# Second attention of a two-layer gated cross-attention kernel: q made transposed, its squares summed by one-column products, a new order in a unit, and the last stage merged into it

## The chip, the cores and the metric

The kernel runs on one core of one Trainium2 chip. The time is the device time of one execution in microseconds; smaller is better. The engines are PE (matrix products), DVE (vector), ACT (activations), POOL (GpSimd) and SP (which only issues transfers here). Each has its own queue of instructions and works it off in order; they wait for one another on semaphores.

## What is computed

Two layers, each a gated cross-attention and a gated feed-forward part, on x of 4 sequences x 256 tokens x 512 features:

```python
x = x + tanh(g_xattn[0]) * L0_xattn(layernorm(x), ctx)       # attn0
x = x + tanh(g_ffn[0])   * L0_ffn(layernorm(x))              # ffn0
x = x + tanh(g_xattn[1]) * L1_xattn(layernorm(x), ctx)       # attn1: changed
x = x + tanh(g_ffn[1])   * L1_ffn(layernorm(x))              # ffn1: moved

def L1_xattn(latents, ctx):                  # 32 heads, 8 key heads, head 128
    kv = concatenate([ctx, latents], 1)      # 64 + 256 keys
    q, k, v = latents @ Wq, kv @ Wk, kv @ Wv
    q, k = rms_norm(q, q_norm_w), rms_norm(k, k_norm_w)     # per head
    return softmax(q @ k.T / sqrt(128)) @ v @ Wo
def L1_ffn(x):                               # 28 experts of rank 8, top 2
    gate = softmax of the two largest of x @ gate_W.T
    return x @ base_W.T + ((x @ lora_A) * gate * 2) @ lora_B
```

All arithmetic is float32. Each operand of a large product is split into a part `hi` that the array's rounded format (fp32r) holds and a rest `lo`, and a product is the sum of three (`mm3`, lines 55 to 57: hi x lo, lo x hi, hi x hi).

## The kernel before

Four phases follow one another; each is a block in which every engine has its own program. The second attention (`attn1_phase`, line 861) has 8 key-head groups g (a loop on every engine, its first and last pass written out) and 4 sequences b, so 32 **units** n = 4g + b. A unit is one sequence with one key head and its four query heads. Units overlap: unit n does its own projections and scores, and in between the value and output products of unit n - 1.

The order of PE within a unit is written by hand (lines 1335 to 1409):

- k and v of 256 tokens, 24 products of 256 columns; for even b also k and v of the context of two sequences, 12 products (`cx`).
- `turn` 0 and 1: transpositions of the unnormalised probabilities p of unit n - 1; then q of the first 128 tokens, 12 products of 512 columns, with tokens as rows and the four heads as columns. `turn` 2 and 3, then q of the other 128 tokens. `turn` 4 and 5. A unit has 20 such 128x128 transpositions.
- `p_v(0)`: p times v for two heads, 8 products of 512 columns; the transpositions of k (2, in even units 3); four transpositions of q (line 1391); `p_v(1)`; the other four of q.
- scores 0 and 1 (12 products of 320 columns), output of the first 128 tokens (`out`, 12 of 512), scores 2, output of the other 128, scores 3.

A pair of scores j stands for 128 query tokens (`tile`) and two heads (`hp`); `PAIRS` gives the order, first both pairs of tile 0.

ACT copies each result out of PSUM as the `hi` part, and DVE subtracts to make the `lo` part, while the bank is held. q with tokens as rows is copied to `q_raw` by ACT (line 1215); DVE squares it and sums each head (`q_squares`, line 1023, eight instructions with a sum each), POOL takes the power -1/2 (lines 970 and 972), and PE transposes `q_raw`. The scale of q enters only in the exponential of ACT (line 1251) as the scale of each row, and in the negative row maximum `nb` (line 1034). k is squared and summed by DVE (line 1071), scaled after POOL's power (lines 964, 966, 1084), and transposed. The probabilities are divided by their sums in `scale_p` (line 1037), for the first pair by POOL (line 957).

The sequence of PSUM banks is fixed by `y_bank` and `x_bank`: two banks take turns for kv, cx, q, p times v and output, two for transposed things. A later product waits until the earlier content of its bank is split, or added into x (`x_add`, line 1013).

DVE and ACT also split the weights of the next group, in the last unit of a group (`w_kv`, `w_q`) and at the end of b = 0 and the start of b = 1 (`w_o`, `w_lo` and `w_hi`). The layer norm of tokens for the next phase is done in the last two units for tiles 0 to 3, and in `tail` for 4 and 5 (`ln_tiles`).

After the last unit, `tail` (line 1411) does the turns, p times v and output that are left. Then the block ends and `ffn1_phase` begins: splits of the base weights and of lora_B (lines 1508 to 1513, 1492), and for each of eight tiles the router and lora_A product (`ag`, 12 products of 256 columns), the base product (12 of 512), the routing on DVE (a chain of some twelve small instructions, lines 1527 to 1543), two transpositions of `hg` and six products of 512 columns with lora_B; DVE adds into x and SP stores.

Of the kernel before, what the change touches and what calls it, by code (L numbers as in the profile page):

```python
# [15 lines left out]


# [6 lines left out]
ALU = mybir.AluOpType  # L24
# [818 lines left out]
def attn1_buffers(k, scope, sb, pair):  # L843
    k.w_q, k.w_o = pair(scope, "w1q", [CH, GH * HD]), pair(scope, "w1o", [GH, HID])
    k.qT = pair(scope, "qT1", [2, GH, PART])
# [8 lines left out]
    k.q_raw, k.k_raw = sb(scope, "q_raw", [2, GH * HD]), sb(scope, "k_raw", [3, HD])  # L854
    k.p1 = sb(scope, "p1", [2, GH, SEQ + CTX])
    k.dump, k.rms_eps = sb(scope, "dump", [2 * GH + 3, HD]), sb(scope, "rms_eps", [2 * GH])
# [4 lines left out]
def attn1_phase(nc, k, sem, ln):  # L861


    def sems(*names):
# [5 lines left out]
    q_full, q_copied, pv_full, pv_hi, pv_split, d_full, x_added = sems(  # L870
        "q_full", "q_copied", "pv_full", "pv_hi", "pv_split", "d_full", "x_added")
    t_full, t_hi, t_split, kt_full, kt_hi, kt_split, qt_full, qt_hi, qt_split = sems(
        "t_full", "t_hi", "t_split", "kt_full", "kt_hi", "kt_split", "qt_full", "qt_hi", "qt_split")
    ssk_ready, rk_ms, rk_ready, k_scaled, ssq_ready, rq_ms, rq_ready = sems(
        "ssk", "rk_ms", "rk", "k_scaled", "ssq", "rq_ms", "rq")
# [7 lines left out]
    PAIRS = [(0, 0), (0, 1), (1, 0), (1, 1)]  # L883
# [18 lines left out]
    def x_bank(b, kind, j=0):  # L902
        at = {"t": j, "k": 6, "q": 7 + j}[kind]
        return bx[(9 * b + at) % 2]
# [7 lines left out]
    def ln_bank(b, i):  # L912
        return bx[(9 * b + 1 + i) % 2] if b < BATCH else bx[i]
# [10 lines left out]
    def stat(j):  # L924
        tile, hp = PAIRS[j]
        return slice(tile * GH + 2 * hp, tile * GH + 2 * hp + 2)

    def piece(kind, i):
        n = cols[kind] // CONV[kind]
        return slice(i * n, (i + 1) * n)  # L930

    def loop(eng, body, tail):

        body(0, True, True)
        with eng.Fori(1, NKV - 1) as g:
            body(g, False, True)
        body(NKV - 1, False, False)
        tail(NKV * BATCH)

    with nc.Block() as block:  # L940
        @block.sync
        def _(sp):
# [4 lines left out]
            for kind in ("kv", "q", "o"):  # L947
                sp.wait_ge(wlo[kind], NKV * CONV[kind])
                k.ffn1_load(sp, kind)

        @block.gpsimd
        def _(pool):
# [7 lines left out]
            def body(g, first, nxt):  # L960
                for b in range(BATCH):
# [8 lines left out]
                    pool.tensor_tensor(k.rq[:, :], k.ssq[:, :], k.rms_eps[:, :], ALU.add).then_inc(rq_ms, 1)  # L970
                    pool.wait_ge(rq_ms, n + 1)
                    pool.tensor_tensor(k.rq[:, :], k.rq[:, :], k.minus_half[:, 0:8], ALU.pow).then_inc(rq_ready, 1)
                    p_scale(n, 0)

            pool.memset(k.rms_eps[:, :], HD * RMS_EPS)
            pool.memset(k.ssk[:, :], 1.0).then_inc(stats_set, 1)
            def tail(n):
                for t in (4, 5):
                    ln.pool_rstd(pool, 3, t)
                for w in k.w_kv:  # L980
                    last = pool.memset(f(w[:, :].rearrange("p (c n) -> p c n", c=CH)[:, :, LR + NEXP:256]), 0.0)
                last.then_inc(k.ag_pad, 1)
# [4 lines left out]
        def _(dve):  # L987
            def w_lo(kind, g, i):
                s = piece(kind, i)
                dve.wait_ge(whi[kind], CONV[kind] * g + i + 1)  # L990
                dve.tensor_tensor(flat[kind][1][:, s], raw[kind][:, s], f(flat[kind][0][:, s]),
                                  ALU.subtract).then_inc(wlo[kind], 1)
# [20 lines left out]
            def x_add(n, b, j):  # L1013
                t = 2 * ((b - 1) % BATCH) + j
# [4 lines left out]
            def q_squares(n, b, tile):  # L1019
                dve.wait_ge(q_copied, 2 * n + tile + 1)  # L1020
                for h in range(GH):
                    q = k.q_raw[:, tile, h * HD:(h + 1) * HD]
                    last = dve.tensor_tensor_reduce(k.dump[:, tile * GH + h, :], q, q, 1.0, 0.0, ALU.mult, ALU.add,
                                                    k.ssq[:, tile * GH + h:tile * GH + h + 1])
                if tile == 1:
                    last.then_inc(ssq_ready, 1)
# [728 lines left out]
```

## Time and profile before

| | |
|---|---|
| median of 3 runs | 1496.01 us (1492.74 to 1496.33) |
| profiled execution, its own time | 1493.15 us |
| its span, first to last instruction | 1491.4 us |
| mean granted clock of PE | 0.992 |
| busy: PE, DVE, ACT, POOL | 1399.5, 1058.6, 798.0, 462.6 us |

The second attention takes from about 574 us to 1436 of the span, its 32 units up to 1410; the last stage the rest. A row of the timeline has the start and the duration in us, engine, line, operation, result and operands with their shape, and in brackets the idle time before it and what ended that. Durations of PE's products overlap. Where a helper issues an instruction, the row has the helper's line: all three-part products stand at lines 55 to 57 and are told apart by the names of their tiles.

### The profile page before, as it was taken

The page shows a single profiled execution, that of the slowest core. Times are in us where ns is not written, and L with a number is a line of the kernel's source. Part 1 is how long each engine was busy: PE and PEld are TensorE (multiplying, and loading weights), DVE is VectorE, ACT ScalarE, POOL GpSimd, SP SyncE. Part 2 cuts the span into 40 slices and gives each one's busy share as a digit, 9 for nine tenths or more (in the row PEclk, how much of TensorE's full clock was granted, in tenths as well). Part 3 has the DMA queues.
Part 4 walks back from the last instruction along what each step waited for, and adds up shares of the span by engine and source line. Part 5 has one row for each costly group of instructions (what it writes and reads, how often), then busy time and mean ns, then how long its engine had stood idle before and what let it go on. Part 6 is the DMA issues. An engine that isn't in the chain of part 4 may idle for free. (4 is left out here: it accounts for less than half of the span.)

```text
span 1491.4 us, 24301 instructions
## 1 busy us (share of the span) xinstructions
PE 1399.5 (94%) x7976; PEld 1199.3 (80%) x7976; DVE 1058.6 (71%) x2794; ACT 798.0 (54%) x2204; POOL 462.6 (31%) x588
## 2 busy tenths in 40 slices
PE   4999999998999998999999999999999999999889
PEld 4888888887778876888878888888888878887767
DVE  6777777778633337787787787787787777787765
ACT  4777777775211315565555555555555555555521
POOL 3855555554954612111111121111211111112120
PEclk8999999999999999999999999999999999999989
DMA  4111122111321301001001001001001000100001
GB/s 191 71 55 60 70 70 70 65 61 44 104 68 43 123 1 71 1 1 72 1 1 71 0 1 71 0 1 71 0 1 71 0 36 35 38 18 1 1 0 57
DMA packets 14958, 63.96 MB, mean 43 GB/s; under 512 B 1760, under 2 KB 1760, under 8 KB 10656
## 3 DMA queue, kind: packets, MB, share of 16 engines
q1 hardware_dynamic: 14880, 63.07, 11.8%
q8 instruction: 30, 0.49, 0.1%
q14 instruction: 48, 0.39, 0.1%
HBM read 60.97 MB, written 2.10 MB: 42 GB/s over the span
## 5 line engine op out<-in xcount | busy, mean ns | idle before, releaser
L1251 ACT ACTIVATE p<-psum,nb,rq 128x320 f32<-128x320 f32 x256 | 155.3, 614 | 161.8 <-DVE nb L1034 161.8
L55 PE MATMUL psum<-w1q_hi,xnT_lo 128*128 128x512 f32 x256 | 107.2, 419 | 12.8 <-DVE v_lo L1054 8.3
L964 POOL TENSOR_TENSOR rk<-ssk,rms_eps 128x3 f32<-128x3 f32 x32 | 6.3, 196 | 349.9 <-DVE ssk L1071 349.9
L999 DVE TENSOR_TENSOR pT_lo<-psum,pT_hi 128x512 fp32r<-128x512 f32 x128 | 88.1, 689 | 32.5 <-ACT pT_hi L1174 30.7
L1030 DVE TENSOR_REDUCE mx<-psum 128x2 f32<-128x640 f32 x128 | 105.0, 820 | 5.7
L1215 ACT ACTIVATE q_raw<-psum 128x512 f32<-128x512 f32 x64 | 38.3, 598 | 121.3 <-PE psum L57 121.3
L361 DVE TENSOR_TENSOR VW_lo<-psum,VW_hi 64x512 fp32r<-64x512 f32 x128 | 88.0, 688 | 19.1 <-ACT VW_hi L457 17.5
L57 PE MATMUL psum<-w1q_hi,xnT_hi 128*128 128x512 f32 x256 | 100.6, 393 | 0.0
L55 PE MATMUL psum<-w1o_hi,oT_lo 128*128 128x512 f32 x256 | 100.4, 392 | 0.0
L56 PE MATMUL psum<-w1o_lo,oT_hi 128*128 128x512 f32 x256 | 100.3, 392 | 0.0
L56 PE MATMUL psum<-w1q_lo,xnT_hi 128*128 128x512 f32 x256 | 99.8, 390 | 0.0
L57 PE MATMUL psum<-w1o_hi,oT_hi 128*128 128x512 f32 x256 | 99.7, 390 | 0.0
L957 POOL TENSOR_TENSOR p<-p,rinv 128x640 f32<-128x640 f32 x32 | 42.7, 1335 | 139.6 <-DVE rinv L1040 139.6
L481 ACT ACTIVATE p<-psum,nb 128x64 f32<-128x64 f32 x256 | 76.8, 318 | 16.7 <-DVE nb L393 16.4
L55 PE MATMUL psum<-w_kv_hi,xnT_lo 128*128 128x256 f32 x288 | 81.7, 284 | 3.1 <-PEq L687 1.8
L55 PE MATMUL psum<-kT_hi,qT_lo 128*128 128x320 f32 x256 | 81.9, 320 | 1.9 <-ACT p L1251 1.0
L1297 PE MATMUL psum<-ident,p 128*128 128x128 f32 x512 | 73.5, 277 | 10.0 <-DVE pT_lo L999 6.2
L457 ACT ACTIVATE VW_hi<-psum 64x512 fp32r<-64x512 f32 x128 | 75.9, 593 | 10.6 <-PE psum L57 8.6
L56 PE MATMUL psum<-w_kv_lo,xnT_hi 128*128 128x256 f32 x288 | 81.5, 283 | 0.0
L57 PE MATMUL psum<-w_kv_hi,xnT_hi 128*128 128x256 f32 x288 | 81.5, 283 | 0.0
L57 PE MATMUL psum<-kT_hi,qT_hi 128*128 128x320 f32 x256 | 79.1, 309 | 0.0
L56 PE MATMUL psum<-kT_lo,qT_hi 128*128 128x320 f32 x256 | 79.0, 309 | 0.0
(245 smaller groups left out, 4676.8 us busy)
## 6 DMA issues: line engine op xcount, KB each, us to landing
raw_q<-in_w0q SPq DMA_DIRECT2D x8, 1024.0 KB, 4.8
raw_o<-in_w0o SPq DMA_DIRECT2D x8, 1024.0 KB, 4.8
raw_q<-in_w1q SPq DMA_DIRECT2D x8, 1024.0 KB, 7.5
raw_o<-in_w1o SPq DMA_DIRECT2D x8, 1024.0 KB, 4.8
raw_kv<-in_w_gu SPq DMA_DIRECT2D x10, 512.0 KB, 3.6
raw_gu<-in_w_gu SPq DMA_DIRECT2D x10, 512.0 KB, 3.6
raw_kv<-in_w0kv SPq DMA_DIRECT2D x8, 515.0 KB, 3.3
raw_kv<-in_w1kv SPq DMA_DIRECT2D x8, 512.0 KB, 5.5
```

Source lines behind the costliest of these rows:

```text
L55: pe.matmul(out, w[1], m[0], start=start, stop=False)
L56: pe.matmul(out, w[0], m[1], start=False, stop=False)
L57: return pe.matmul(out, w[0], m[0], start=False, stop=stop)
L361: last = dve.tensor_tensor(k.VW[1][r, h // 2, 2 * pr + bp, :], bank[64 * bp:64 * bp + 64, :], f(k.VW[0][r, h // 2, 2 * pr + bp, :]), ALU.s ...
L457: last = act.activation(k.VW[0][r, h // 2, 2 * pr + bp, :], bank[64 * bp:64 * bp + 64, :], ACT.Copy)
L481: last = act.activation(k.p0[:, s % 4, h * CTX:(h + 1) * CTX], s_bank[s % 2][:, h * CTX:(h + 1) * CTX], ACT.Exp, bias=k.nb0[:, s % 2, h:h ...
L957: pool.tensor_tensor(p, p, k.rinv[:, stat(j)].unsqueeze(2).to_broadcast([PART, 2, KEYS]), ALU.mult).then_inc(p_scaled_pool, 1)
L999: last = dve.tensor_tensor(k.pT[1][:, kt, 2 * hp:2 * hp + 2, :], bank.rearrange("p (h q) -> p h q", h=2), f(k.pT[0][:, kt, 2 * hp:2 * hp + ...
L1030: dve.tensor_reduce(k.mx[:, stat(j)], s_pair(j), AX.X, ALU.max).then_inc(mx_ready, 1)
L1215: act.activation(k.q_raw[:, j // 2, :], y_bank(b, "q", j // 2)[:, :], ACT.Copy)\
L1251: last = act.activation(k.p1[:, tile, h, :], s_pair(j)[:, h % 2, :], ACT.Exp, bias=k.nb[:, i:i + 1], scale=k.rq[:, i:i + 1], accum_out=k.r ...
L1297: last = pe.transpose(bank[:, (2 * hh + tile) * PART:(2 * hh + tile + 1) * PART], k.p1[:, tile, 2 * hp + hh, CTX * hh + kt * PART:CTX * hh ...
```

## The change

In the second attention:

- **q is made transposed.** The weights of a head are now the stationary operand and the tokens move: 48 products of 256 columns for the 24 of 512 (`q_proj`), by pairs of heads. ACT copies the result straight to `qT` hi (`q_hi`), DVE makes `qT` lo (`q_lo`). `q_raw`, its copy, the eight transpositions of q and DVE's eight squares are gone.
- **Squares.** ACT squares the PSUM bank into `q_sq` (f32, `q_square`), after `qT` lo is made. Eight products with a column of ones (128 x 128 of `q_sq` stationary, one column moved, plain f32) sum them into eight columns of a bank. DVE adds the epsilon, POOL's addition goes and its power stays.
- **Order.** The transpositions of k come after the first half of q, with turns 2 behind them; then the second half of q, turns 3 and 4, `p_v(0)`, turn 5, the one-column products, scores 0 and 1, `p_v(1)`, scores 2, output of the first tokens, scores 3, output of the others. `PAIRS` now has both tiles of the first two heads first. `x_add` of the second output moves to the head of the next unit's DVE program. The splits of `w_o` stand together at the head of b = 1. `out` waits for the halves of `oT` one by one.
- **End.** `ffn1` becomes a class whose steps stand in `tail` among the steps of the last unit. Its weights and tiles lie in buffers of the attention. The router weights and base weights are split in the last unit as a ninth group's; POOL splits lora_B. One bank each for `ag` and transposed `hg`, where there were two. Tiles 6 and 7 are normalised in the tail too.

```diff
-    PAIRS = [(0, 0), (0, 1), (1, 0), (1, 1)]
+    PAIRS = [(0, 0), (1, 0), (0, 1), (1, 1)]
...
+            def q_lo(n, b, hp):
+                dve.wait_ge(qt_hi, 2 * n + hp + 1)
+                dve.tensor_tensor(k.qT[1][:, 2 * hp:2 * hp + 2, :],
+                                  y_bank(b, "q", hp)[:, :].rearrange("p (h q) -> p h q", h=2),
+                                  f(k.qT[0][:, 2 * hp:2 * hp + 2, :]), ALU.subtract).then_inc(qt_split, 1)
...
                     n, prev = BATCH * g + b, not (first and b == 0)
+                    if not (first and b < 2):
+                        x_add(n - 1, b - 1, 1)
+                    if b == 1:
+                        for i in range(CONV["o"]):
+                            w_lo("o", g, i)
...
+                    dve.wait_ge(ssq_full, n + 1)
+                    dve.tensor_scalar(k.ssq[:, :], x_bank(b, "ssq")[:, 0:2 * GH], HD * RMS_EPS, None,
+                                      ALU.add).then_inc(ssq_ready, 1)
...
+            def q_square(n, b, hp):
+                act.wait_ge(qt_split, 2 * n + hp + 1)
+                act.activation(k.q_sq[:, hp, :], y_bank(b, "q", hp)[:, :], ACT.Square).then_inc(q_squared, 1)
...
+                        for hh in range(2):
+                            h = 2 * hp + hh
+                            for c in range(CH):
+                                last = mm3(pe, y_bank(b, "q", hp)[:, hh * SEQ:(hh + 1) * SEQ],
+                                           [w[:, c, h * HD:(h + 1) * HD] for w in k.w_q],
+                                           [w[:, c, b * SEQ:(b + 1) * SEQ] for w in k.xnT], c == 0, c == CH - 1)
                         last.then_inc(q_full, 1)
+
                     if prev:
-                        turn(n, b, 4)
-                        turn(n, b, 5)
-                        p_v(n, b, 0)
-                        pe.wait_ge(t_split, 6 * (n - 1) + 5)
+                        turn(n, b, 0)
+                        turn(n, b, 1)
+                    q_proj(0)
+                    if prev:
+                        pe.wait_ge(t_split, 6 * (n - 1) + 1)
                     pe.wait_ge(k_scaled, n + 1)
                     nk = 3 if b % 2 == 0 else 2
                     for i in range(nk):
                         last = pe.transpose(x_bank(b, "k")[:, i * PART:(i + 1) * PART], k.k_raw[:, i, :], k.ident[:, :])
                     last.then_inc(kt_full, 1)
...
+                    if prev:
+                        turn(n, b, 2)
+                    q_proj(1)
+                    if prev:
+                        turn(n, b, 3)
+                        turn(n, b, 4)
+                        p_v(n, b, 0)
+                        turn(n, b, 5)
+                        pe.wait_ge(t_split, 6 * (n - 1) + 5)
+                    else:
+                        pe.wait_ge(stats_set, 1)
+                    pe.wait_ge(q_squared, 2 * n + 2)
+                    for j, (tile, hp) in enumerate(PAIRS):
+                        for hh in range(2):
+                            at = hh * SEQ + tile * PART
+                            last = pe.matmul(x_bank(b, "ssq")[:, 2 * j + hh:2 * j + hh + 1], k.q_sq[:, hp, at:at + PART],
+                                             k.one[:, :], start=True, stop=True)
+                    last.then_inc(ssq_full, 1)
                     scores(n, b, 0)
                     scores(n, b, 1)
...
             def tail(n):
...
+                ffn1.pe_ag(pe, 0)
+                turn(n, 0, 0, alone=True)
+                turn(n, 0, 1, alone=True)
+                ffn1.pe_ag(pe, 1)
+                ffn1.pe_base(pe, 0)
...
+                p_v(n, 0, 0, alone=True)
+                ffn1.pe_ag(pe, 2)
+                p_v(n, 0, 1, alone=True)
+                ffn1.pe_base(pe, 2)
+                ffn1.pe_hgT(pe, 0)
+                out(n, 0, 0)
+                ffn1.pe_low_rank(pe, 0)
...
+                for s in range(3, NT):
...
+                    ffn1.pe_ag(pe, s)
+                    ffn1.pe_hgT(pe, s - 1)
+                    ffn1.pe_base(pe, s)
+                    if s < NT - 1:
+                        ffn1.pe_low_rank(pe, s - 1)
```

## Rows read from the trace of the kernel before

**Rows 1.** Page, part 1: busy us (share), instructions of each engine
```profile
PE 1399.5 (94%) x7976; PEld 1199.3 (80%) x7976; DVE 1058.6 (71%) x2794; ACT 798.0 (54%) x2204; POOL 462.6 (31%) x588
```

**Rows 2.** Stages: length, busy us of PE, PEld, DVE, ACT, POOL, clock, DMA share, GB/s
```profile
1000.00:1100.00 100.00, 96.80 (x561) 83.12 (x559) 77.06 (x237) 56.40 (x145) 14.65 (x18) 1.00 0.07 27
...
1400.00:1440.00 40.00, 28.18 (x127) 21.75 (x126) 24.44 (x45) 14.68 (x35) 3.83 (x12) 0.87 0.00 0
1440.00:1492.00 52.00, 47.75 (x252) 40.47 (x252) 32.96 (x130) 10.41 (x35) 5.01 (x10) 0.97 0.11 41
```

**Rows 3.** Timeline of PE: the first product of five units (b = 2, 3, 0, 1, 2)
```profile
922.87 0.28 PE L55 MATMUL psum<-w_kv_hi,xnT_lo 128*128 128x256 f32 x1
...
950.60 0.28 PE L55 MATMUL psum<-w_kv_hi,xnT_lo 128*128 128x256 f32 x1
...
976.01 0.28 PE L55 MATMUL psum<-w_kv_hi,xnT_lo 128*128 128x256 f32 x1
...
1004.74 0.28 PE L55 MATMUL psum<-w_kv_hi,xnT_lo 128*128 128x256 f32 x1
...
1030.13 0.28 PE L55 MATMUL psum<-w_kv_hi,xnT_lo 128*128 128x256 f32 x1
```

**Rows 4.** Timeline of PE within the unit that starts at 922.87
```profile
925.63 0.28 PE L57 MATMUL psum<-w_kv_hi,xnT_hi 128*128 128x256 f32 x1
...
927.19 1.04 PE L1297 MATMUL psum<-ident,p 128*128 128x128 f32 x8
...
928.29 0.39 PE L56 MATMUL psum<-w1q_lo,xnT_hi 128*128 128x512 f32 x1
...
929.91 0.40 PE L57 MATMUL psum<-w1q_hi,xnT_hi 128*128 128x512 f32 x1
930.68 0.50 PE L55 MATMUL psum<-w1q_hi,xnT_lo 128*128 128x512 f32 x1 [0.37 <-DVE pT_lo L999]
```

**Rows 5.** Waits of PE from 640 to 1400 us: us in total, times, longest
```profile
PE psum L55 <- DVE v_lo L1054: 8.3, 5, 1.7
PE psum L1297 <- DVE pT_lo L999: 5.0, 9, 1.7
PE psum L1391 <- DVE pT_hi L1003: 3.7, 9, 0.6
PE psum L55 <- DVE pT_lo L999: 3.4, 9, 0.4
```

**Rows 6.** Timeline of all engines in the unit that starts at 976.01 (b = 0)
```profile
980.21 0.28 PE L57 MATMUL psum<-w_kv_hi,ctxT_hi 128*128 128x256 f32 x1
...
980.70 1.11 ACT L1203 ACTIVATE v_hi<-psum 64x128 fp32r<-64x128 f32 x4
...
982.52 0.42 DVE L1054 TENSOR_TENSOR v_lo<-psum,v_hi 128x256 fp32r<-128x256 f32 x1 [2.29 <-issue]
...
983.00 0.50 PE L55 MATMUL psum<-w1q_hi,xnT_lo 128*128 128x512 f32 x1 [1.64 <-DVE v_lo L1054]
...
985.76 0.85 POOL L966 TENSOR_TENSOR rk<-rk,minus_half 128x3 f32<-128x3 f32 x1
...
986.64 0.68 DVE L1084 TENSOR_SCALAR k_raw<-k_raw,rk 128x128 f32<-128x128 f32 x3 [0.64 <-POOL rk L966]
```

**Rows 7.** Timeline of PE from the last scores to the last product
```profile
1409.55 0.31 PE L57 MATMUL psum<-kT_hi,qT_hi 128*128 128x320 f32 x1
...
1423.83 0.80 PE L55 MATMUL psum<-pT_hi,v_lo 128*128 128x512 f32 x1 [2.90 <-DVE pT_hi L1003]
...
1487.74 0.40 PE L57 MATMUL psum<-w_b_hi,hgT_hi 96*128 96x512 f32 x1
```

**Rows 8.** Groups by line, 680 to 1360 us: count, busy us, mean ns, idle before
```profile
L972 POOL TENSOR_TENSOR rq<-rq,minus_half 128x8 f32<-128x8 f32 x25 | 40.9, 1637 | 2.0
...
L1215 ACT ACTIVATE q_raw<-psum 128x512 f32<-128x512 f32 x51 | 30.5, 598 | 97.4 <-PE psum L57 97.4
...
L1023 DVE CUSTOM_DVE_ANT_0 dump<-q_raw 128x128 f32<-128x128 f32 x200 | 46.2, 286 | 0.8
```

More of the change, by code:

```diff
@@ L938, in loop @@
         tail(NKV * BATCH)
+    ffn1 = Ffn1(k, sem, ln, free={"kv": kv_wlo, "q": q_wlo, "exp": exp_done, "scores": s_full, "w_kv": kv_full,
+                                  "turned": t_split, "x": x_added, "whi": kv_whi}, conv=CONV, units=UNITS)
     with nc.Block() as block:
@@ L1192, in body @@
                     n, prev = BATCH * g + b, not (first and b == 0)
-                    split_next = b == BATCH - 1 and nxt
+                    split_next = b == BATCH - 1
+                    if b == 1:
+                        if not first:
+                            act.wait_ge(d_full, 2 * (n - 1))
+                        for i in range(CONV["o"]):
+                            w_hi("o", g, i)
                     act.wait_ge(kv_full, n + 1)
@@ L1225, in body @@
+                    for late in ln_tiles(n):
+                        ln.act_norm(act, *late)
                     if split_next:
                         w_hi("q", g + 1, 0)
[L1227 to L1236 removed]
@@ L1330, in scores @@
                 for hh in range(2):
[L1331 removed]
+                    last = mm3(pe, s_pair(j)[:, hh, :], [w[:, 2 * hp + hh, tile * PART:(tile + 1) * PART] for w in k.qT],
                                [w[:, b, CTX * (1 - hh):CTX * (1 - hh) + KEYS] for w in k.kT], True, True)
@@ L1405, in body @@
                         out(n, b, 0)
-                    scores(n, b, 2)
+                    if ln_tiles(n):
+                        pe.wait_ge(ssq_ready, n + 1)
+                    for i, tile in enumerate(ln_tiles(n)):
+                        ln.pe_turn(pe, *tile, ln_bank(b, i))
+                    scores(n, b, 3)
                     if prev:
                         out(n, b, 1)
-                    scores(n, b, 3)
             def tail(n):
-                for j in range(6):
-                    turn(n, 0, j, alone=True)
-                    if j == 3:
-                        pe.wait_ge(x_added, 2 * (n - 1))
-                        p_v(n, 0, 0, alone=True)
@@ L1417, in tail @@
-                p_v(n, 0, 1, alone=True)
-                for i in range(2):
-                    ln.pe_turn(pe, 3, 4 + i, ln_bank(4, i))
-                for j in range(2):
-                    out(n, 0, j)
+                ffn1.pe_ag(pe, 0)
[3 more added lines that the diff above has]
+                ffn1.pe_base(pe, 0)
+                turn(n, 0, 2, alone=True)
+                turn(n, 0, 3, alone=True)
+                ffn1.pe_base(pe, 1)
@@ L1626, in build @@
+def build(nc, d, out):
     k = Kernel()
```

733 lines of the change are left out of this document (362 added, 371 removed).

## The prediction, made before the change was run

> **What bounds the kernel now.** I read the shares of busy time first: PE is busy for 94% of the span, DVE for 71% [rows 1]. The table by stage then separates two regimes. In the second attention PE is busy for 97 of 100 us at the full clock of 2.4 GHz; in the last 92 us it is busy for only 76, and the first 40 of them run at a mean granted clock of 0.87 [rows 2]. So PE's own instructions set the time of the 32 units, and in the end waits do. The timeline of PE gives the length of a unit: 27.73 us for b = 2, 25.41 for b = 3, 28.73 for b = 0, 25.39 for b = 1 [rows 3], some 107 us for four.
>
> **What one PE instruction costs** is its distance to the next start, not its duration, since they overlap. 256 columns: (925.63 - 922.87)/23 = 0.120 us. 512 columns: (929.91 - 928.29)/7 = 0.231. A 128-column transposition: the eight last 1.04 us with the 0.28 of a single one in it, so 0.76/7 = 0.109, and 927.19 to 928.29 is eight of these and one 512-column product, with nothing over [rows 3, 4]. For 320 columns I interpolate 0.148.
>
> **PE's work in a unit.** q made transposed takes 48 products of 256 columns for 24 of 512: 5.76 for 5.54 us, +0.22, or **+7 us** over 32 units. This is on the path, because PE is. The eight transpositions of q go: 8 x 0.109 = 0.87 us, **-28 us**. The eight one-column products come. The trace has no product of that shape. Each loads 128 columns of weights from a plain f32 tile and moves one column. The nearest row is the transposition, which also loads 128 columns of f32; its 0.109 us can't be for its 128 moved columns alone, as 256 columns fewer save only 0.111, that is 0.055 per 128. So the cheap end is 0.05 each (-15 us against the value I take), the near row is 0.109, and the dearest PE instruction of the trace, 0.231, is the dear end: 8 x 0.122 x 32 = 31 us more. I take 0.109, **+28 us**, as nothing but the moved columns differs in shape; but the transposition only moves data, and this product multiplies plain f32, which no row shows. The Trainium skill (FP8 and Floating Point Precision, Matmul Precision, under TensorE Precision Notes) says that true FP32 takes four passes through the array, while the kernel's other products are rounded f32 in one. An estimate by that rule is four times the term, 112 us and not 28; no row here shows such a product.
>
> **Waits of PE in the units, before.** The longest in the list are 8.3 + 5.0 + 3.7 + 3.4 = 20.4 us in 32 waits, over 28 units [rows 5]. A wait costs more than its idle time: 929.91 to 930.68 is 0.77, less the usual 0.23 is 0.54, where the row says 0.37 [rows 4]. With 0.17 for each: 25.8 us, 30 over 32 units. By difference: an odd unit's work is 2.88 (kv) + 20 x 0.109 + 5.54 + 10 x 0.109 + 40 x 0.231 (values and output) + 24 x 0.148 = 24.5 us, so 0.9 of 25.4 is lost; an even one has 1.44 + 0.11 more work, so b = 2 loses 1.7 and b = 0 2.7; 6.2 in four units, 50 over 32. The difference also catches waits too short to leave an idle row; I take 43, nearer to it.
>
> **Waits of PE in the units, after.** (a) Keys early. The transpositions of k now come after two turns of p and q's first half: 8 x 0.109 + 24 x 0.120 = 3.75 us behind the last context product of an even unit. What they need is a chain: context product at 980.21, ACT's copies of v from 980.70 over 1.11 us, to 981.8; then DVE's four subtractions (1.2) and three squares with their sums (0.7), to 983.7; POOL 0.1 + 0.2 + 0.85, to 984.9; the scaling, 0.68, to 985.6 [rows 6]. With 0.1 for the last signal that is 5.5 us behind the start of that product at 980.21, against 0.12 + 3.75 = 3.9 for PE. PE waits 1.6 us in 16 even units: 26 us. Before, twelve more products, turns and a p times v lay in between and hid it. In an odd unit the chain starts from the kv products and ends as PE arrives. (b) The loop of DVE. At each new group of four DVE stands 2.29 us ahead of its first subtraction, and PE 1.64 us for its result [rows 6]. The second half of the output now comes last, 2.8 us behind the last scores, so DVE ends its unit earlier by that; but the sum into x for it has moved across the loop's edge. PE asks for it ahead of the context product, 2.9 us into the unit. DVE's last scaling ends at 1.0, the standing makes it 3.3, the sum 4.0: 1.2 us in 8 units, 10 us. Past that the subtraction is in time. (c) Row scale. The sum of squares is ready only at the first scores; DVE 0.2, POOL's power 1.64 [rows 8], the maximum's product 0.2, two exponentials 1.3, signals 0.5: 3.9 us. PE covers 12 x 0.148 + 8 x 0.231 = 3.6 ahead of the third scores, so it loses 0.2 in each unit, 6 us. Together 42 us: **-1 us**.
>
> **Costed at nothing.** DVE loses eight squares of 286 ns a unit [rows 8]; it isn't the bound, and that slack is what makes (c) no dearer. ACT squares from PSUM where it copied to SBUF, both 128x512, 598 ns [rows 8], twice; PE's wait for the second square is covered by the turns of p and the first p times v (3.6 us against 2.3 of copies). The split of w_o moves whole to the head of b = 1: four copies of ACT, 2.2 us, end before kv is there at 2.9. The queue of SP keeps its loads in order and each has a group (107 us) to land. **The three units that also turn layer-norm tiles** take them behind the output product, where their banks have long been free; I give 1 us each, **-3 us**.
>
> **The end.** From the last scores at 1409.55 to the last product at 1487.74 it takes 78.2 us, with a wait of 2.90 for one pT alone [rows 7]. The work in it, at the full clock: router and low-rank in 96 x 0.120 = 11.5, base 96 x 0.231 = 22.2, low-rank out 48 x 0.231 = 11.1, 52 transpositions 5.7, p times v and output 40 x 0.231 = 9.2: 59.7 us. The merged order puts the first three tiles' products between the turns of the last unit, and removes the block's edge and the split of the base weights, which goes into the last unit. I leave 6.5 us of waits: DVE has some 18 us of subtractions and routing for the 19 of PE ahead of the last output, starts 3 us later, and one bank each for router and hgT puts more handshakes in. So 66 us, **-12 us**.
>
> **Sum.** +7 - 28 + 28 - 1 - 3 - 12 = -9 us on the profiled execution's 1493.15, so 1484. That execution lies 3 us below the median of the three runs, 1496.01, and at the foot of their spread; a median after should lie above its profiled run too, and I put it at 1486.
>
> **Rivals.** One: *nothing in the way.* One-column products at 0.05, the waits at (a) half as long because DVE's copies pack closer: 1486 - 15 - 13 = 1458 for both, about 1472 for either. For: the transposition row leaves 0.05 for the load. Against: signals usually add. 10%. Two: *keys early eats the rest.* The k chain has ACT's turns of p behind it and DVE's in its middle; if the two turns of p that DVE does ahead of the scaling run late by 0.7 us (ACT must copy both after v), (a) is 2.3 us, 11 us more: 1497, no change. For: the copy of the second turn ends only 0.2 us before DVE wants it. Against: POOL's power hides it. 12%. Three, on the other side: *the one-column products take several passes.* The place is PE between the turns and the first scores, with nothing beside it; the price per pass is a load of 0.109. Two passes: 8 x 0.109 x 32 = 28 us more, 1514; four: 84 more, 1570. It decides from 0.148 us a product (10 us over 256 above 0.109), and is slower beyond doubt from 0.166. For: the tile is plain f32, where all products of the trace are fp32r and split in two by hand; against: PE's list has one load to each f32 transposition. 34%, two parts in three of it for two passes.
>
> **Chances.** The forecast, 1486, 44%, with a range of its own from 1477 to 1494 (the half-known terms, waits and end, at 4 us each side). About 0.3%, or 4.5 us, is what a measurement of this kernel can tell from no change. Faster is below 1491.5: 42 of the forecast, 10 of rival one and 1 of two, 53%. Same: 2 of the forecast and 9 of rival two, 11%. Slower: 34 and 2, 36%. The range 1466 to 1522 takes in the forecast, most of rival one, rival two and two passes (1514 and 8 for its waits), and leaves out four passes (11%) and the fastest few.
>
> **What the profile after will show.** If the step on products holds, the eight start 0.11 us apart and their line has 256 executions in all; loads in a multiple of that, or 0.2 us and more, are rival three. The transpositions of k start 5.5 us behind the last context product in even units, with k_raw named as what they wait for; if that idle time is above 2 us it is rival two. The first subtraction of each group still shows a standing of about 2 us, and the context product waits for x. From the last scores to the last product some 66 us, with no stretch at 1.2 GHz. I am wrong if even units are not longer by a few tenths, odd ones not shorter, or if the end is shorter by less than 6 or more than 18 us.

## The result, and the profile after

The changed kernel takes 1506.05 us (median of four runs, 1504.21 to 1508.01) against 1495.35 for the kernel before on the same chip (1492.74 to 1496.33): ratio 1.0077, interval 1.0060 to 1.0094. It is **slower by 0.8%**; the forecast was 1486, 0.6% faster. The profiled execution of after took 1508.01 us (span 1506.2), that of before 1493.15 (span 1491.4), so the traces are to explain +14.8.

The page's part 1 for the changed kernel, against [rows 1]:

```profile
PE 1423.9 (95%) x9000; PEld 1280.2 (85%) x9000; DVE 1001.0 (66%) x2314; ACT 800.7 (53%) x2210; POOL 453.9 (30%) x559
```

DVE sheds 58 us and stays far from bounding. PE has 1024 more instructions. By the code a unit gains 24 products of q, loses eight transpositions and gains eight one-column products: 24 more, 768 in 32 units. The 256 left over are eight a unit. PE's groups by line (680 to 1360 us, 25 units), every shape apart, show whose they are:

```profile
L1353 PE MATMUL psum<-ident,p 128*128 128x128 f32 x392 | 50.8, 273 | 0.0
L1455 PE MATMUL psum<-one,q_sq 128*128 128x1 f32 x400 | 46.2, 245 | 0.0
```

400 executions in 25 units are 16 a unit, where the code issues eight. The turns of p (L1353), 16 a unit by the code, have one record each (392, where a few are missing). PE's timeline of the even unit that starts at 1048.20 says what that is worth:

```profile
1052.51 1.03 PE L1353 MATMUL psum<-ident,p 128*128 128x128 f32 x8
...
1058.03 0.52 PE L1438 MATMUL psum<-ident,k_raw 128*128 128x128 f32 x3 [1.62 <-DVE k_raw L1086]
...
1064.20 0.38 PE L1348 MATMUL psum<-ident,p 128*128 128x128 f32 x2
1064.42 1.85 PE L1455 MATMUL psum<-one,q_sq 128*128 128x1 f32 x16
...
1077.23 0.28 PE L57 MATMUL psum<-w_kv_hi,xnT_lo 128*128 128x256 f32 x1
```

The eight products begin at 1064.42 and the scores behind them at 1066.13: 1.71 us, 0.214 a product and 0.107 a record. That is rival three with two passes. The second thing to see is the 1.62 in front of the turned keys. PE's waits from 640 to 1400 us, against [rows 5]:

```profile
PE psum L1438 <- DVE k_raw L1086: 22.7, 14, 1.6
PE psum L1348 <- DVE pT_lo L1008: 0.3, 1, 0.3
PE psum L1455 <- DVE pT_lo L1008: 0.2, 1, 0.2
```

All listed waits of before are gone, and a new one of 1.6 us stands in each even unit. Its total, 22.7, is a little more than that of the four of before (20.4).

**Where the 14.8 us lie**, by the first product of each unit. The attention starts 2.3 us earlier. Units 0 and 1 take 27.3 and 31.3 us for 19.6 and 28.6: +10.4. Units 2 to 29 take 766.1 for 748.6: +17.6; in their steady part a group of four is 29.02 + 25.68 + 29.02 + 25.68 = 109.40 for 107.26, +0.54 a unit. Units 30 and 31 take 33.8 and 31.1 for 30.9 and 27.9: +5.9. The end behind them takes 64.8 for 81.7: -16.9. Together +14.7.

The first and last units also lost clock. Stretches of after: length, busy us of PE and the granted clock, two of unit 0, two of unit 30, one of unit 31:

```profile
560.00:570.00 10.00, 5.59 (x43) 0.95 0.00 0
570.00:580.00 10.00, 8.97 (x49) 0.71 0.00 0
1394.00:1398.00 4.00, 4.00 (x22) 0.64 0.02 4
1398.00:1402.00 4.00, 4.00 (x13) 0.51 0.00 0
1424.00:1430.00 6.00, 5.77 (x29) 0.65 0.00 0
```

1.00 is 2.4 GHz and 0.50 is 1.2; a value between is the mean of a stretch with both. Before, these units ran at 1.00 and the falls, 13.7 us at 0.50 in all, came in the end [rows 2]. Units 0 and 1 of after have three falls, each in a wait or right behind one: at 551.99 behind a wait of 1.83 for the attention's first product, at 569.05, only 0.3 us into the one-column products and behind a wait of 2.16, and at 589.53 inside the wait of 4.05. The waits of the two units:

```profile
563.18 0.55 PE L1438 MATMUL psum<-ident,k_raw 128*128 128x128 f32 x3 [2.25 <-DVE k_raw L1086]
...
568.75 3.27 PE L1455 MATMUL psum<-one,q_sq 128*128 128x1 f32 x16 [2.16 <-ACT q_sq L1218]
...
576.45 0.39 PE L57 MATMUL psum<-kT_hi,qT_lo 128*128 128x320 f32 x1 [1.03 <-ACT p L1286]
...
590.00 0.66 PE L1438 MATMUL psum<-ident,k_raw 128*128 128x128 f32 x2 [4.05 <-DVE k_raw L1086]
```

In units 30 and 31 the clock fell at 1395.08 and 1425.80, 1.5 and 1.1 us behind the first one-column product, with waits of 0.25 and 0.92 us shortly before. Experiment 2, with one product for the eight, has falls in units 0 and 1 as well and none in units 30 and 31. So the first ones don't need the one-column products, and the last ones go with them. They don't come every time: the trace of experiment 8 has the same 16 records in each unit and no fall in units 30 and 31.

### The profile page after: what moved, and what is told of

The parts are those of the page before. It is cut to its first block, busy times and chain, and to the rows that moved or that the text cites. A ratio compares the mean times of both kernels' runs of the same rounds, so it can differ in the third digit from the quotient of the medians.

```text
span 1506.2 us, 25804 instructions
## 1 busy us (share of the span) xinstructions
PE 1423.9 (95%) x9000; PEld 1280.2 (85%) x9000; DVE 1001.0 (66%) x2314; ACT 800.7 (53%) x2210; POOL 453.9 (30%) x559
## 4 chain that ended last, share of the span: by engine, by line
PE 54%; DVE 6%; ACT 2%; issue 1%; POOL 0%; DVEq 0%; ACTq 0%
PE psum L57 15%; PE psum L59 14%; PE psum L58 14%; PE psum L1455 4%; PE psum L1353 3%; PE psum L1367 2%; DVE pT_lo L1008 2%; DVE v_lo L1072 1%; ACT v_hi L1243 1%; PE psum L1348 1%; PE psum L1438 1%; DVE dump L1078 1%; DVE k_raw L1086 1%; ACT p L1286 0%; DVE mx L1037 0%
## 5 line engine op out<-in xcount | busy, mean ns | idle before, releaser
L57 PE MATMUL psum<-xnT_hi,w1q_lo 128*128 128x256 f32 x512 | 150.4, 294 | 0.0
L59 PE MATMUL psum<-xnT_hi,w1q_hi 128*128 128x256 f32 x512 | 145.0, 283 | 0.0
L58 PE MATMUL psum<-xnT_lo,w1q_hi 128*128 128x256 f32 x512 | 145.0, 283 | 0.0
L983 POOL TENSOR_TENSOR rq<-ssq,minus_half 128x8 f32<-128x8 f32 x32 | 52.4, 1637 | 278.0 <-DVE ssq L1116 278.0
L58 PEld LDWEIGHTS psum<-xnT_lo,w1q_hi 128*128 128x128 f32 x512 | 98.5, 192 | 0.0
L57 PEld LDWEIGHTS psum<-xnT_hi,w1q_lo 128*128 128x128 f32 x512 | 98.4, 192 | 0.1
L59 PEld LDWEIGHTS psum<-xnT_hi,w1q_hi 128*128 128x128 f32 x512 | 98.2, 192 | 0.0
L57 PE MATMUL psum<-kT_hi,qT_lo 128*128 128x320 f32 x256 | 86.9, 339 | 1.0 <-ACT p L1286 1.0
L1008 DVE TENSOR_TENSOR pT_lo<-psum,pT_hi 128x512 fp32r<-128x512 f32 x128 | 82.1, 682 | 1.9 <-ACT pT_hi L1200 1.4
```

Source lines behind the costliest of these rows:

```text
L57: pe.matmul(out, w[1], m[0], start=start, stop=False)
L58: pe.matmul(out, w[0], m[1], start=False, stop=False)
L59: return pe.matmul(out, w[0], m[0], start=False, stop=stop)
L983: pool.tensor_tensor(k.rq[:, :], k.ssq[:, :], k.minus_half[:, 0:8], ALU.pow).then_inc(rq_ready, 1)
L1008: last = dve.tensor_tensor(k.pT[1][:, kt, 2 * hp:2 * hp + 2, :], bank.rearrange("p (h q) -> p h q", h=2), f(k.pT[0][:, kt, 2 * hp:2 * hp + ...
```

## The experiments

Medians below are of four to ten runs; ratios are to the kernel before on the same chip.

**1. One pass.** The squares and the ones become fp32r, with two equal columns moved instead of one.

```diff
-    k.q_sq, k.k_raw = sb(scope, "q_sq", [2, 2 * SEQ]), sb(scope, "k_raw", [3, HD])
+    k.q_sq, k.k_raw = sb(scope, "q_sq", [2, 2 * SEQ], F32R), sb(scope, "k_raw", [3, HD])
...
-                            last = pe.matmul(x_bank(b, "ssq")[:, 2 * j + hh:2 * j + hh + 1], k.q_sq[:, hp, at:at + PART],
+                            last = pe.matmul(x_bank(b, "ssq")[:, 4 * j + 2 * hh:4 * j + 2 * hh + 2], k.q_sq[:, hp, at:at + PART],
```

> The changed kernel with the squares written as fp32r and the eight products in that type, two columns moved for one (the sum stands in the first). Routing tiles of the last stage lie in another buffer, at no cost. Theory A (each plain f32 product is two passes, 16 starts 0.107 us apart, and nothing beside them hides it): one record for each product, 8 x 0.107 = 0.86 us in a unit for 1.71, so 27 us less over 32 units, about 1479 where the changed kernel has 1506; some us more if the clock holds in the first and last units. Rival B (the products stand in a wait that is there anyway, for the sums or for p): under 8 us less. Rival C (the type makes no difference to the passes): no change.

Measured: 1481.22 us, ratio 0.9909 (0.9893 to 0.9926), ahead of the kernel before by 0.9%. PE's timeline of that kernel:

```profile
1052.94 1.04 PE L1455 MATMUL psum<-one,q_sq 128*128 128x2 f32 x8
```

Eight records, 0.90 us to the scores where it was 1.71. The units are 25.00 and 28.37 long, -0.67 each, which is 18.7 us in units 2 to 29. Units 30 and 31 give 6.2, a good part of it clock (one fall in place of two longer ones), and units 0 and 1 give 1.4. The second pass alone is the sign of the result. This run changed the type and moved two columns for one; experiment 2 tells the two apart.

**2. One product for the eight.** Seven of the eight sums of squares are left out.

```diff
-                    for j, (tile, hp) in enumerate(PAIRS):
-                        for hh in range(2):
...
+                    last = pe.matmul(x_bank(b, "ssq")[:, 0:2 * GH], k.q_sq[:, 1, 0:PART], k.ident[:, 0:2 * GH], start=True, stop=True)
```

> The changed kernel with one product of eight columns (f32, the identity's first columns moved) in place of the eight one-column products; left out: seven of the eight sums of squares, so the scale of q is not the reference's. Theory A: 2 starts for 16, 14 x 0.107 = 1.5 us less in a unit, 48 us less over 32, about 1458. Clock theory (in units 0, 1, 30 and 31 the clock falls to 1.2 GHz because the products move almost no columns next to a wait): granted clock 1.00 in the last two units and their length back to 29 and 26 less 1.5, which is 8 us more, 1450. Rival B (waits take the place): under 20 us less in all, and idle rows of PE before scores.

Measured: 1478.42 us, 0.9891 (0.9875 to 0.9908), far from the theory's 1458 and only 2.8 below experiment 1, with the same units, 25.00 and 28.35. Its product moves eight columns of the identity in plain f32 and still leaves two records, so the number of moved columns isn't what makes them; a transposition against the same identity leaves one. PE's timeline of the product:

```profile
1025.02 0.29 PE L1452 MATMUL psum<-ident,q_sq 128*128 128x8 f32 x2
```

The list of PE's waits says why so little is gained:

```profile
PE psum L1438 <- DVE k_raw L1086: 22.7, 14, 1.6
PE psum L57 <- ACT p L1286: 10.2, 27, 0.4
PE psum L57 <- DVE pT_hi L1012: 4.1, 24, 0.2
```

What the products free, the third scores wait for: they go into the bank that the first exponential reads. Experiment 1 stands on the same floor: from the last product of `p_v(0)` to the third scores it takes 5.25 us there, 5.23 here and 5.91 in the changed kernel. So a still cheaper sum of squares is worth nothing by itself. Experiment 7 asks what the floor is.

**3. Twice.** The eight one-column products are issued a second time, behind the first eight.

```diff
-                    for j, (tile, hp) in enumerate(PAIRS):
...
+                    for again in range(2):
+                        for j, (tile, hp) in enumerate(PAIRS):
...
+                                last = pe.matmul(x_bank(b, "ssq")[:, 2 * j + hh:2 * j + hh + 1], k.q_sq[:, hp, at:at + PART],
+                                                 k.one[:, :], start=True, stop=True)
```

> The changed kernel with every one-column product issued twice into the same column; nothing is left out. Theory A: 16 more starts of 0.107 us, 1.71 us more in a unit, 55 us more over 32, about 1561. Clock theory: more than that where the clock falls, and perhaps a fall in the steady units too, where a quiet stretch of 3.4 us now stands (the scores after it then take twice 1.8 us: up to 60 us more again). Rival B: under 30 us more, the rest in waits that are there anyway.

Measured: 1588.54 us, 1.0611 (1.0561 to 1.0662), 82 us above the changed kernel where the price alone gave 55. The four times lie between 1580.32 and 1601.73, and the trace is of the longest. Where the clock holds, the units are 27.47 and 30.82 long, +1.80 or 0.224 a product: the same price again. Other units take 28.8, 30.4, 32.2 and 33.8, because the clock now falls in the steady part as well, each time within or just behind a train of 32 records. Stretches of that kernel, busy us of PE and of its loads, DVE, ACT and POOL, then the clock:

```profile
640.00:800.00 160.00, 156.75 (x999) 146.59 (x999) 96.58 (x242) 77.05 (x197) 21.34 (x21) 0.91 0.05 18
...
960.00:1120.00 160.00, 155.12 (x1070) 144.79 (x1070) 102.30 (x262) 82.06 (x213) 20.75 (x22) 0.98 0.08 33
```

A PE that counts as busy for 98% of a stretch gets 0.91 of the clock there. The share of busy time doesn't show this loss; the granted clock has to be read beside it.

**4. The end alone**: the kernel before with the merged end and nothing else of the change. DVE's part of it, against the kernel before, begins:

```diff
-                for j in range(4):
-                    t_lo(n, 0, j)
+                ffn1.dve_iota(dve)
+                ffn1.dve_top(dve, 0)
+                t_lo(n, 0, 0)
+                t_lo(n, 0, 1)
+                ffn1.dve_gates(dve, 0)
...
```

> The kernel before, with the merged end alone: its own order in a unit, q with tokens as rows, eight transpositions of q. By the traces the end after the last scores' unit is 16.9 us shorter in the changed kernel, at equal work. Theory A: the end's gain stands by itself, 13 to 17 us less than the kernel before, about 1480, and this beats both kernels. Rival D: part of the gain hangs on the new order (probabilities of the first two heads ready early, output last), then 4 to 9 us less.

Measured: 1481.29 us, 0.992 (0.9892 to 0.9948). The merged end is worth some 14 us by itself (8 to 16 by the interval), in a kernel whose steady units are as before. What stands behind the last unit is 13.5 us shorter, and units 30 and 31 are 2.8 us longer. So the rest of the change costs some 24 us, and the end pays back about half of it.

**5. Keys later.** In even units PE makes 12 of the second 24 products of q ahead of the turned keys.

```diff
+                    if b % 2 == 0:
+                        q_proj(1, (0,))
                     if prev:
                         pe.wait_ge(t_split, 6 * (n - 1) + 1)
...
-                    q_proj(1)
+                    q_proj(1, (1,) if b % 2 == 0 else (0, 1))
```

> The changed kernel, but in the 16 even units PE makes 12 of the 24 products of the second pair of heads of q before the keys are turned instead of after them; 12 such products take 1.44 us. Theory (the 1.6 us for which the first transposition of the keys waits in an even unit, 22.7 us over 14 of them, are lost on the path): 16 x 1.4 = about 22 us come back, less what the later keys make wait in turn; the scores come 12 us behind, so nothing, and the turns behind q at most 0.4 us a unit: 1484 to 1490 against 1506. Even units 27.6 us long instead of 29.0, odd ones unchanged at 25.7. Rival (the wait only moves, to the turns of the split keys or to the scores, since VectorE is what is late): even units still 29.0, the time within 3 us of 1506.

Measured: 1500.69 us, 1.0038 (1.0026 to 1.0051); even units 28.73 for 29.02. The theory fell. PE's waits:

```profile
PE psum L1353 <- DVE kT_lo L1095: 7.9, 14, 0.6
PE psum L1442 <- DVE k_raw L1086: 2.6, 14, 0.2
PE psum L1353 <- DVE pT_hi L1012: 2.4, 14, 0.2
```

The wait on k_raw shrinks from 22.7 to 2.6. But the split of kT and that of the next p, which DVE makes behind it, come no earlier, and the turns of p need both. The wait moved 12 products down the queue. The keys are turned at the same time as in the changed kernel (9.8 us into the unit), ACT's copies of kT follow and then DVE's split, and 12 products cover that less well than 24. What bounds the even unit here is the chain of the keys over POOL, DVE, PE and ACT, and not their place in PE's queue.

**6. Both**: one pass, and the keys later.

> Both repairs together: the one-column products in one pass (rounded squares, 1481 us alone) and the keys turned 12 products later in the even units. Theory (two separate costs on the path): 1481 - 16 to 22 = 1459 to 1465 us, which would be ahead of both kernels by about 2%; even units 27.0 us. Rival (what the keys' wait frees is eaten by the chain from the scores over the row maximum to the exponential, whose waits stood at 0.4 us a unit once the products were cheap): 1475 or above, with the wait on p grown from 0.7 us to some 16.

Measured: 1474.88 us, 0.9858 (0.9842 to 0.9874). Even units 28.06 for 28.37, again 0.3, which is 4.2 of the 8.1 us between the two traces. Unit 0 goes from 27.7 to 23.9, but unit 1 from 29.5 to 31.6, so the two give 1.7, and units 30 and 31 give 1.3 with no fall of the clock. The theory of two costs that add, 1459 to 1465, fell. The time is the rival's bound, but its sign, a wait on p grown to 16 us, is not there: 0.7 us over 3, as in experiment 1. The wait went to kT, as in experiment 5.

**7. No power.** Experiment 2 with POOL's power replaced by a cheap product; the row scale then holds another number.

```diff
-                    pool.tensor_tensor(k.rq[:, :], k.ssq[:, :], k.minus_half[:, 0:8], ALU.pow)
+                    pool.tensor_tensor(k.rq[:, :], k.ssq[:, :], k.ssq[:, :], ALU.mult)
```

> The kernel with one product for the eight one-column ones (1478 us; seven of eight sums of squares are left out), and GpSimd's power (1.64 us, the row scale) replaced by one cheap product, so the row scale holds another number. It asks what held that kernel at 1478 where the missing products alone would have given about 1458. If it is the power, which ends at the same moment as VectorE's row maximum of the first scores: 0.4 us on the exponential and 0.2 on the transposed p go, over 31 units 10 to 20 us, 1458 to 1468. If it is the chain from the first scores over the row maximum and the exponential alone: 1475 to 1480, no change, the waits on p as before (10.2 us over 27).

Measured: 1479.77 us, 0.9885 (0.9868 to 0.9901), the same as experiment 2 within its spread, with the waits on p at 10.1 us over 27. The power alone is not the floor. Experiment 2's timeline shows DVE's queue without a gap from the split of `oT` to the row maximum, the exponential behind it and the third scores behind that:

```profile
1025.63 0.69 DVE L1018 TENSOR_TENSOR oT_lo<-psum,oT_hi 128x512 fp32r<-128x512 f32 x1 [0.84 <-ACT oT_hi L1208]
1026.23 0.16 DVE L1116 TENSOR_SCALAR ssq<-psum 128x8 f32<-128x8 f32 x1
1026.42 0.86 DVE L1012 TENSOR_TENSOR pT_hi<-psum,pT_hi 64x256 fp32r<-64x256 f32 x2
1026.47 1.64 POOL L983 TENSOR_TENSOR rq<-ssq,minus_half 128x8 f32<-128x8 f32 x1 [8.52 <-DVE ssq L1116]
1027.31 0.82 DVE L1037 TENSOR_REDUCE mx<-psum 128x2 f32<-128x640 f32 x1
...
1028.24 0.16 DVE L1041 SCALAR_TENSOR_TENSOR nb<-mx,rq 128x2 f32<-128x2 f32 x1
...
1028.44 0.62 ACT L1286 ACTIVATE p<-psum,nb,rq 128x320 f32<-128x320 f32 x1 [2.19 <-DVE nb L1041]
...
1029.80 0.42 PE L57 MATMUL psum<-kT_hi,qT_lo 128*128 128x320 f32 x1 [0.38 <-ACT p L1286]
```

The power ends at 1028.11 and the maximum at 1028.13: taking either away leaves the other. The first scores are not what the maximum waits for. Their six products start from 1025.16 to 1025.98, and DVE takes them up at 1027.31, right behind its splits. That queue starts with the result of `p_v(0)`, which DVE gets from ACT at 1025.6. In the changed kernel the long train of one-column products gives DVE the time to be done with the split of `oT` first (it then stands 0.58 us for the sums). That DVE's queue is the limit is read from the timeline; it was not tried by shortening it.

**8. VectorE's order.** In even units DVE takes two squares of k ahead of the split of the context's values, and the second split of p behind the scale of k. PE's order is untouched.

```diff
                     if b % 2 == 0:
+                        for i in range(2):
+                            dve.tensor_tensor_reduce(k.dump[:, 2 * GH + i, :], k.k_raw[:, i, :], k.k_raw[:, i, :], 1.0, 0.0,
...
                         dve.wait_ge(cx_hi, 2 * g + b // 2 + 1)
...
                         t_lo(n, b, 0)
-                        t_lo(n, b, 1)
+                        if b % 2:
+                            t_lo(n, b, 1)
...
                     last.then_inc(k_scaled, 1)
+                    if prev and b % 2 == 0:
+                        t_lo(n, b, 1)
```

> The changed kernel with another order on VectorE in the even units alone, PE's order untouched: the squares of the two key tiles of x go ahead of the split of the context's values (which waits 1.64 us for ScalarE anyway), and the split of the second transposed p goes behind the scale of the keys. Both stand ahead of the scale now: 2 x 0.22 and 0.6 us. Theory (the keys' wait of 1.6 us in an even unit is VectorE's order, and the later keys only gained 0.3 because the same late split of kT came next): the scale is ready about 1.0 us earlier and everything behind it too: waits of PE on k_raw 22.7 us to about 8, even units 28.0 instead of 29.0, 1490 us against 1506. Rival (the wait is handed on to the turns of the transposed p, as with the later keys): even units 28.7, 1501 or above.

Measured: 1499.73 us, 1.0036 (1.0023 to 1.0049). Even units 28.81, waits of PE:

```profile
PE psum L1444 <- DVE k_raw L1090: 16.8, 14, 1.2
```

0.4 us of the 1.6 went, not 1.0, and the unit gained only half of that, 0.21. Of the 6 us to the changed kernel some 3 are in the even units; in the trace units 30 and 31, with no fall of the clock, are 6.2 us shorter together. The timeline of an even unit shows what took over:

```profile
1054.52 0.29 DVE L1081 CUSTOM_DVE_ANT_0 dump<-k_raw 128x128 f32<-128x128 f32 x1
...
1054.85 0.69 DVE L1008 TENSOR_TENSOR pT_lo<-psum,pT_hi 128x512 fp32r<-128x512 f32 x1
1056.05 0.68 DVE L1090 TENSOR_SCALAR k_raw<-k_raw,rk 128x128 f32<-128x128 f32 x3 [0.51 <-POOL rk L979]
1056.65 0.68 DVE L1008 TENSOR_TENSOR pT_lo<-psum,pT_hi 128x512 fp32r<-128x512 f32 x1
1056.88 0.52 PE L1444 MATMUL psum<-ident,k_raw 128*128 128x128 f32 x3 [1.19 <-DVE k_raw L1090]
1057.38 0.44 PE L1354 MATMUL psum<-ident,p 128*128 128x128 f32 x2
```

The last square ends at 1054.81 and POOL's scale is there at 1056.0. DVE now stands 0.51 us for POOL, which the split of the second p had covered. That split now ends at 1057.33, and by the code `turn` 2 on PE needs it: it starts 0.50 us behind the turned keys, where it was 0.36 in the changed kernel. This small wait has no row of its own and takes back most of the other 0.2.

**9 and 10. The new order with one pass, and with the keys later as well.**

> The same order on VectorE with the one-column products in one pass (1481 us without it). Theory: the two costs add, 1481 - 16 = 1465 us, even units 27.4. Rival (the gain is handed on to the scores' chain): 1475 or above.

> One pass, VectorE's new order and the keys turned 12 products later in the even units (1474.9 us without the new order). Theory (with the scale 1.0 us earlier the later keys wait for nothing, and the split of kT, 0.75 and 0.42 us late in 16 units, is early enough): even units 26.9 instead of 28.06, 1474.9 - 17 = 1458 us. Rival (the turns wait on pT as before): 1470 or above.

Measured: 1477.22 us, 0.9874 (0.9853 to 0.9896), even units 28.16; and 1469.48 us, 0.9828 (0.9804 to 0.9852), even units 27.70. The first is its rival's time and the second comes out at its rival's bound: neither reaches the sum of the single gains. Unit 0 is 22.8 us long in the second trace, with one fall of the clock. Later keys gain 0.46 in an even unit with the new order and 0.3 without it; the turns still wait for the split of kT:

```profile
PE psum L1359 <- DVE kT_lo L1101: 5.8, 14, 0.4
PE psum L1359 <- DVE pT_hi L1012: 2.4, 14, 0.2
```

**11. All squares first.** Over experiment 10, the context's keys are signalled on their own and their square goes ahead of the split of the values too.

```diff
-                        act.activation(k.k_raw[:, 2, :], y_bank(b, "cx")[:, 0:HD], ACT.Copy)
+                        act.activation(k.k_raw[:, 2, :], y_bank(b, "cx")[:, 0:HD], ACT.Copy).then_inc(cx_hi, 1)
...
+                                dve.wait_ge(cx_hi, 2 * (2 * g + b // 2) + 1)
```

> The kernel with all three repairs (1469.5 us), and in the even units the square of the context's keys too ahead of the split of its values, so that GpSimd's row scale of the keys (1.3 us after the squares, and 0.51 us late for VectorE in the run with the new order alone) starts 1.4 us earlier. Theory (the keys' chain runs from the squares over GpSimd to the scale): the scale is ready 0.5 us earlier, so is the split of kT, for which the turns waited 0.4 us in 14 units, and the q products ahead of it; even units 27.2 instead of 27.7, 1462 us. Rival (the split of kT waits for ScalarE and the turned keys, not for VectorE): even units 27.6, 1468 or above.

Measured: 1469.05 us, 0.9817 (0.9790 to 0.9844), even units 27.69 for 27.70. The rival holds. Its timeline of an even unit shows why:

```profile
1037.50 0.67 DVE L1094 TENSOR_SCALAR k_raw<-k_raw,rk 128x128 f32<-128x128 f32 x3
...
1039.35 0.49 PE L1452 MATMUL psum<-ident,k_raw 128*128 128x128 f32 x3
...
1039.87 0.47 ACT L1262 ACTIVATE kT_hi<-psum,qkw 128x256 fp32r<-128x256 f32 x1 [1.17 <-PE psum L1452]
...
1040.89 0.48 DVE L1101 SCALAR_TENSOR_TENSOR kT_lo<-psum,qkw,kT_hi 128x256 fp32r<-128x256 f32 x1 [1.47 <-ACT kT_hi L1265]
...
1042.04 0.63 PE L1363 MATMUL psum<-ident,p 128*128 128x128 f32 x4 [0.56 <-DVE kT_lo L1105]
```

The keys are scaled at 1038.17, and PE turns them only 1.2 us later, where its queue has them. ACT stands 1.17 us for the turned keys and DVE 1.47 us for ACT's copies: neither queue is late, the chain from the turned keys to the turns of p is 2.7 us long and PE has too little to do in it. So the order of experiment 5 now holds back what the earlier squares gained. The squares first with the keys turned earlier again was not tried. What remains, 27.7 against the 25.0 of an odd unit, is 1.55 of work for the context and some 1.1 lost, of which 0.56 and 0.17 stand as waits in front of these turns.

The last two kernels beat both others: 1.8% under the kernel before, 2.5% under the changed one. Unit 0 of the last trace is 26.3 us long against 22.8 in that of experiment 10, with PE's order the same and a longer stretch at 1.2 GHz: part of what the first units gain or lose from run to run is the clock.

## Why the prediction was wrong

**The step that failed is the one-column product.** "I take 0.109, +28 us" took the transposition's price, because "nothing but the moved columns differs in shape". The trace shows 0.214, two records of 0.107 to each product of plain f32: 8 x 0.214 x 32 = 55 us in place of 28. Experiment 1 takes the second pass away and gets 25 us back, experiment 3 pays the 0.22 again. With 27 us more the sum is 1484 + 27 = 1511, against 1508.01 for the profiled execution, so the other errors, listed below, nearly cancelled, which is luck. The text had the weak point ("multiplies plain f32, which no row shows"), had the time by it (1514) and gave it 34%. What tipped the choice was likeness of shape, where the kind of product was what mattered: transposition and sum stand in the trace with the same type and the same weights, and only the second leaves two records. The Trainium skill (FP8 and Floating Point Precision, TensorE Precision Notes) says that true FP32 takes four passes. That it takes more than one points the right way; four don't agree with the two records and 0.214 us here.

**Keys early (a) held to the tenth.** 1.6 us in each even unit but unit 0, which has 2.25; 22.7 us over the 14 in the list. The chain was right link by link: the keys' turn starts 5.6 us behind the last context product. In odd units PE finds the keys ready, as said, except in unit 1, where it waits 4.05 us. What I did not see is that the chain goes on behind the turned keys: experiment 5 shows that moving them alone gets back only 0.3 of the 1.6.

**The loop of DVE (b) did not come.** Units with b = 0 and b = 2 are equally long (29.02). DVE's sum into x at a group's head starts 1.32 us into the unit, behind the split of w_q, with no standing before it:

```profile
994.24 0.68 DVE L1053 TENSOR_SCALAR p<-p,rinv 128x320 f32<-128x320 f32 x2
994.84 0.75 DVE L1026 SCALAR_TENSOR_TENSOR x<-psum,gate,x 128x512 f32<-128x512 f32 x1
997.28 0.42 DVE L1066 TENSOR_TENSOR v_lo<-psum,v_hi 128x256 fp32r<-128x256 f32 x1 [1.70 <-ACT v_hi L1237]
```

If the 2.29 us of [rows 6] stand anywhere they are inside the 1.70 that ends with ACT. Why they did not come before the sum stays open. The step had 10 us too many.

**The row scale (c)** was taken at 0.2 a unit. With two passes there was no such wait at all, with one pass it is 0.7 us over three units, and only the kernel with a single product shows the chain (0.4). In the long train ahead of the scores DVE gets through the splits that stand before its maximum (experiment 7): 6 us too many.

**q transposed** was nearly right: 24 products of q take 2.95 us with their joints, 48 take 5.9 for the 5.76 of the text, 4 us too few over 32 units. Without their second pass (experiment 1) four units are 106.74 long, for 107.26 before; the sum of the steps had +0.19 a unit and got -0.13, mostly by (b) and (c).

**The three units with layer-norm tiles** were given -3 us and units 0, 30 and 31 cost +13.6, unit 1 another 2.7. I gave unit 0 no chain of its own. It has no p to turn, so the keys, the squares and the exponential are waited for in the open (2.25, 2.16 and 1.03 us), and the clock falls there, as in all the traces of this order. In units 30 and 31 most of the loss goes with the clock: with one pass they are 30.0 and 28.6 long, the first of them wholly at 1.00, and in experiment 8, with both passes and no fall, 30.4 and 28.2.

**The end** was -12 and came out at -16.9 (-13.5 alone, experiment 4, beside the units of before). All of it runs at the full clock, where the end before had 13.7 us at 1.2 GHz, so part of the 16.9 is clock. The listed waits of PE are 0.9 and 0.7 us only, against [rows 7]. I had left 6.5 us of waits in it; stretch of after, 60.0 of 64.6 us busy:

```profile
1441.43:1506.00 64.57, 59.99 (x333) 51.00 (x331) 44.76 (x155) 18.92 (x54) 6.16 (x18) 1.00 0.09 33
```

## What to carry to other kernels

Price an operation that the trace lacks by its arithmetic before its shape: a row of the same tile sizes that only moves data is no measure of one that multiplies plain f32, and where one form of the data (here squares in fp32r) avoids the question, use it. Before moving a late consumer down the queue, look at what its producer does next; here the wait travelled with it, and 1.6 us of wait were worth 0.3. After an earlier link has been made faster, ask again whether the consumer still stands where it should. And time the parts of a change apart: the merged end alone was worth some 14 us, and the sum of both hid it.

## What the runs showed of the hardware

A product of plain f32 weights (128x128) with one moved column leaves two records of 0.107 us, each with its load of weights; with eight moved columns it leaves two as well (experiment 2). The fp32r one with two columns leaves one, 0.112 apart. A transposition of plain f32 leaves one record of 0.109.

The granted clock fell to 0.50 in waits of 1.8 to 4.1 us or right behind them (units 0 and 1), though not in the kernel before, which has the same wait of 1.8 us at the attention's start. It also fell within trains of one-column products with short waits before them (units 30 and 31), in places where PE counted as wholly busy (4.00 of 4.00 us at 0.51). With twice as many such products it fell in steady units too, 0.91 over 160 us. In experiment 1 it stayed at 1.00 in unit 30, and in experiment 8, with all sixteen records, too. In unit 30 of the changed kernel the twelve first scores took 3.35 us, in a steady unit 1.84.
